# Eight experts' second product as three fp32r terms, with both operands split into a high and a low part

## The reference

```python
topw, topi = jax.lax.top_k(router_weights, K)          # K = 2 of E = 8 experts per token
h = jax.nn.gelu(jnp.einsum('td,edf->etf', xf, w1) + b1[:, None, :], approximate=False)
eo = jnp.einsum('etf,efd->etd', h, w2) + b2[:, None, :]  # the experts' second product
out = jnp.einsum('etd,te->td', eo, combine)
```

## Time and profile before

| | |
|---|---|
| median of 3 runs | 2344.29 us (2343.64 to 2345.33) |
| the profiled execution | 2352.8 us |
| its span, first to last instruction | 2351.0 us |
| stage B within the span | about 1401 to 1922 us |
| TensorE, VectorE, ScalarE, GpSimd busy | 91%, 64%, 46%, 41% of the span |
| mean granted TensorE clock | 0.98 |

### The profile page before, as it was taken

The page is one execution under the profiler, slowest core; times in us unless marked ns, Lnnn a source line. Parts: engine busy times, 40 slices in busy tenths (PEclk is TensorE's granted clock), DMA queues, the critical chain, the costliest instruction groups (busy, mean ns, idle before and its releaser), DMA issues.

```text
span 2351.0 us, 81509 instructions
## 1 busy us (share of the span) xinstructions
PE 2131.1 (91%) x31188; PEld 1835.3 (78%) x31189; DVE 1514.2 (64%) x3179; ACT 1086.2 (46%) x2772; POOL 961.8 (41%) x1190
## 2 busy tenths in 40 slices
PE   5999999999999999999999939999999977888887
PEld 4878877878878778778778739999999965666665
DVE  4687787787787886887877851111111127999997
ACT  2354354454454453543543525555555534444444
POOL 3445455454554553654654531000000015656663
PEclk9999999999999999999999969999999999999999
DMA  8401001001001010010000044111111121111110
GB/s 201 152 3 39 10 18 41 11 19 35 16 19 31 20 32 13 20 37 8 21 21 6 19 143 142 36 36 36 38 36 36 36 61 47 57 47 54 56 52 18
DMA packets 93810, 101.00 MB, mean 43 GB/s; under 512 B 24304, under 2 KB 84720, under 8 KB 93424
## 3 DMA queue, kind: packets, MB, share of 16 engines
q1 hardware_dynamic: 83728, 69.93, 9.9%
q0 software_dynamic: 9440, 27.29, 3.6%
q10 hardware_dynamic: 384, 0.01, 0.0%
HBM read 64.95 MB, written 32.24 MB: 41 GB/s over the span
## 4 chain that ended last, share of the span: by engine, by line
PE 54%; issue 17%; DVE 14%; POOL 6%; ACT 5%; SPq 1%; DMA 1%; DVEq 1%; POOLq 0%; ACTq 0%
PE ps_scores L1049 11%; PE ps_w L1059 10%; PE ps_o L875 7%; PE ps_scores L836 4%; ACT pt_all L1202 4%; PE ps_qk L723 4%; PE ps_qk L757 3%; PE ps_xv L663 2%; DVE rs L1448 2%; PE ps_xv L741 2%; DVE lower L1429 2%; POOL lower L1857 2%; POOL rstd L1873 1%; PE ps_scores L783 1%; PE ps_scores L843 1%
## 5 line engine op out<-in xcount | busy, mean ns | idle before, releaser
L1441 DVE TENSOR_REDUCE mb<-ps_scores 128x16 bf16<-128x2048 f32 x160 | 365.8, 2286 | 43.8 <-PE ps_scores L816 39.8
L1956 POOL DMA_INDIRECT arena<-sorted_y,pidx x64 | 63.9, 998 | 609.1 <-ACT pidx L1313 584.4
L1448 DVE RECIPROCAL rs<-ps_o 128x256 f32<-128x256 f32 x160 | 280.4, 1753 | 31.3 <-PE ps_o L875 27.2
L1202 ACT ACTIVATE pt_all<-ps_scores 128x512 f32<-128x512 f32 x512 | 264.2, 603 | 65.2 <-PE ps_scores L843 63.4
L1049 PEld LDWEIGHTS ps_scores<-tiles,w_now 128*128 128x128 f32 x2272 | 266.1, 193 | 5.4 <-issue 1.8
L1049 PE MATMUL ps_scores<-tiles,w_now 128*128 128x128 f32 x2272 | 266.6, 276 | 1.2 <-DVE tiles L1717 1.2
L1287 ACT ACTIVATE tiles<-ps_scores,b1s 128x128 f32<-128x128 f32 x568 | 154.5, 383 | 238.4 <-PE ps_w L1059 230.9
L1059 PE MATMUL ps_w<-arena,tiles 128*128 x1136 | 257.0, 379 | 2.5 <-ACT tiles L1287 2.5
L1059 PEld LDWEIGHTS ps_w<-arena,tiles 128*128 128x128 f32 x1136 | 210.3, 190 | 28.6 <-issue 2.9
L1873 POOL TENSOR_TENSOR rstd<-ve,neghalf 128x1 f32<-128x1 f32 x192 | 109.9, 572 | 274.1 <-DVE ve L1459 266.3
L1857 POOL TENSOR_TENSOR lower<-lower,consts 128x512 fp32r<-128x512 f32 x160 | 171.3, 1070 | 117.9 <-DVE lower L1429 77.6
(11 more groups left out here) (233 smaller groups left out, 4531.5 us busy)
## 6 DMA issues: line engine op xcount, KB each, us to landing
tiles<-sorted_x SPq DMA_DIRECT2D x72, 128.0 KB, 2.0
sorted_y<-tiles SPq DMA_DIRECT2D x71, 128.0 KB, 1.7
w_experts<-in_L_xattn_e_w SPq DMA_DIRECT2D x6, 1024.0 KB, 11.7
arena<-in_L_xattn_e_w POOLq DMA_DIRECT2D x12, 384.0 KB, 4.1
ct_scratch<-cT SPq DMA_DIRECT2D x32, 128.0 KB, 1.7
x_scratch<-x2b_all SPq DMA_DIRECT2D x32, 128.0 KB, 1.8
arena<-x_scratch SPq DMA_DIRECT2D x32, 128.0 KB
cT<-ct_scratch SPq DMA_DIRECT2D x32, 128.0 KB, 2.1
```

Source lines behind the costliest of these rows:

```text
L1202: nc.scalar.activation(pt[:, 4 * g:4 * g + 4, :].rearrange("p h q -> p (h q)"), ps_s[:, g, :], ACT.Exp, bias=bias, scale=LAYER[l]["scale"] ...
L1441: V.tensor_reduce(mb[:].rearrange("p (g r) -> p g r", g=BANKS)[:, :, 0:SLOTS], ps_s[:].rearrange("p g (h k) -> p g h k", h=SLOTS), AX_X, A ...
L1448: V.reciprocal(rs[:], ps_o[:, 2:4, :]).then_inc(recip_ready, 1)
```

## The change

Each operand of the second product becomes a sum of two fp32r numbers, high and low. A product is then high times high, plus high times low of the weights, plus low times high of the weights; low times low is left out. `down` has 24 fp32r matmuls for the 8 fp32 ones.

- Inner values: per tile, `tile_split` on VectorE makes `g_split` with two copies (the high halves) and two subtractions (the low halves), each of 128x512 elements.
- Second weights: per expert, `split_w2` on GpSimd makes the two parts with 4 copies of 128x512 and 8 subtractions of 128x256. The source is one raw buffer, the target a ring of two experts. From expert 2 on, GpSimd waits until the last tile that used this half of the ring is behind (`upto`).
- `hidden` waits for the split of the tile before, where it waited for its `down`.
- The raw weights of expert 0 are loaded inside stage A's last iteration. Those of expert e+1 are loaded when expert e is split.
- The first weights of experts 6 and 7 are loaded from SyncE's queue, between the first tile loads.
- The table has three more instructions (which half of the ring, which first weights to wait for, how many tiles up to each expert).

```diff
         def down(k):
             e = pe.value_load(tbi[0:1, 1, bass.ds(k, 1)], min_val=0, max_val=E - 1)
-            wait(pe, ld_experts, e * 48 + 16)
-            wait(pe, b_gelu, k + 1)
+            odd = pe.value_load(tbi[0:1, 3, bass.ds(k, 1)], min_val=0, max_val=1)
+            wait(pe, w2_ready, e + 1)
+            wait(pe, b_split, k + 1)
             wait(pe, b_y, k)
             for j in range(FC):
-                last = mm(ps_w[:, 0:D], gT[:, j, :], w2f[:, bass.ds(e * (FC * D) + j * D, D)], start=j == 0, stop=j == FC - 1)
+                for g_, w_ in ((0, 0), (0, 1), (1, 0)):
+                    last = mm(ps_w[:, 0:D], g_split[:, g_, j, :].bitcast(F32R),
+                              w2_split[:, bass.ds(odd * (2 * FC * D) + (w_ * FC + j) * D, D)].bitcast(F32R),
+                              start=j == 0 and g_ + w_ == 0, stop=j == FC - 1 and g_ == 1)
             last.then_inc(b_down, 1)
...
+        pe.wait_ge(table_step, TABLE_PAR)
...
         def hidden(k, par):
             wait(act, b_up, k + 1)
             wait(act, b_b1, k + 1)
-            wait(act, b_down, k)
+            wait(act, b_split, k)
...
+        def tile_split(k):
+            wait(dve, b_gelu, k + 1)
+            wait(dve, b_down, k)
+            half = FC // 2
+            for h in range(2):
+                V.tensor_copy(g_split[:, 0, half * h:half * (h + 1), :].bitcast(F32R), gT[:, half * h:half * (h + 1), :]).then_inc(b_high, 1)
+            for h in range(2):
+                wait_apart(dve, b_high, 2 * k + h + 1)
+                last = V.tensor_tensor(g_split[:, 1, half * h:half * (h + 1), :].bitcast(F32R), gT[:, half * h:half * (h + 1), :],
+                                       g_split[:, 0, half * h:half * (h + 1), :], ALU.subtract)
+            last.then_inc(b_split, 1)
...
                 tile_y(k - 1, (d - 1) % 2, j)
+                tile_split(k)
...
+        def split_w2(e):
+
+            pool.wait_ge(ld_w2, 16 * (e + 1))
+            if e >= 2:
+                tiles_ = pool.value_load(upto[0:1, e - 2:e - 1], min_val=1, max_val=TILES + 1)
+                wait_apart(pool, b_split, tiles_)
+            at_ = (e % 2) * 2 * FC * D
+            for j in range(0, FC, 2):
+                G.tensor_copy(w2_split[:, at_ + j * D:at_ + (j + 2) * D].bitcast(F32R), w2_raw[:, j * D:(j + 2) * D]).then_inc(w2_high, 1)
+            for j in range(FC):
+                if j % 2 == 0:
+                    pool.wait_ge(w2_high, FC // 2 * e + j // 2 + 1)
+                last = G.tensor_tensor(w2_split[:, at_ + (FC + j) * D:at_ + (FC + j + 1) * D].bitcast(F32R), w2_raw[:, j * D:(j + 1) * D],
+                                       w2_split[:, at_ + j * D:at_ + (j + 1) * D], ALU.subtract)
+            last.then_inc(w2_ready, 1)
+            pool.wait_ge(w2_ready, e + 1)
+
+        split_w2(0)
+        load_w2(1)
+        split_w2(1)
+        pool.wait_ge(table_step, TABLE_PAR)
         for e in range(2, E):
-            for j0, j1 in ((0, 3), (3, 6), (6, FC)):
-                load_w2(e, j0, j1)
-            pool.wait_ge(ld_experts, 16 + 48 * e)
+            load_w2(e)
+            split_w2(e)
```

SyncE's queue (the first weights of experts 6 and 7), and GpSimd's early load:

```diff
         load_tile(0, 0)
         load_tile(1, 1)
+        for s in range(NS):
+            sp.wait_ge(x2_stored[s], 16 * ITERS)
+        load_w1(W1_EARLY)
...
         tile_pair(0, True)
+        for e in range(W1_EARLY + 1, E):
+            sp.wait_ge(ld_w1, 16 * e)
+            load_w1(e)
...
+            if last and tau == TPI - 7:
+
+                pool.wait_ge(wo_ready, NT - 2 * NS)
+                pool.dma_start(w2_raw[:].rearrange("p (j n) -> p j n", j=FC),
+                               a["L2_xattn_e_w2"][0].rearrange("(j p) n -> p j n", p=P)).then_inc(ld_w2, 16)
```

More of the change, by code:

```diff
@@ L127, in program @@
     x2b_all = sb("x2b_all", [2816])
+    with nc.sbuf_tensor("w2_raw", [P, FC * D], F32) as w2_raw, nc.sbuf_tensor("w2_split", [P, 2 * 2 * FC * D], F32) as w2_split, \
+            nc.sbuf_tensor("g_split", [P, 2, FC, P], F32) as g_split:
+        pass
     arena = sb("arena", [16384])
@@ L198, in program @@
     w1f = w1[:].rearrange("p e c n -> p (e c n)")
-    w2f = arena[:, :]
     cv = Carver(arena)
@@ L288, in program @@
     tb = xT_all[:].rearrange("p a b c -> p (a b c)")[:, 0:5 * TILES].rearrange("p (a b) -> p a b", a=5)
-    tbi = sb("tbi", [3, TILES + 1], I32)
+    tbi = sb("tbi", [5, TILES + 1], I32)
+    upto = sb("upto", [E], I32)
     tails = sb("tails", [E], I32)
@@ L309, in program @@
     ld_w1 = sem("ld_w1")
-    ld_experts = sem("ld_experts")
+    ld_w2 = sem("ld_w2")
+    w2_ready = sem("w2_ready")
+    w2_high = sem("w2_high")
+    b_high = sem("b_high")
+    b_split = sem("b_split")
     ld_b2 = sem("ld_b2")
@@ L597, in _, with load_w1 @@
         load_tile(1, 1)
+        def load_w1(e):
+            sp.dma_start(w1[:, e], a["L2_xattn_e_w1"][e].rearrange("(c p) n -> p c n", p=P)).then_inc(ld_w1, 16)
+        for s in range(NS):
+            sp.wait_ge(x2_stored[s], 16 * ITERS)
+        load_w1(W1_EARLY)
         def tile_pair(j, first):
@@ L620, in _ @@
         sp.wait_ge(b_down, TILES)
+        sp.wait_ge(w2_ready, E)
         sp.dma_start(win_f, a["consts"][:, C_WIN:C_ALL]).then_inc(ld_window, 16)
@@ L1276, in copy_weights @@
             e = act.value_load(tbi[0:1, 1, bass.ds(k, 1)], min_val=0, max_val=E - 1)
-            wait(act, ld_experts, e * 48 + 16)
+            late = act.value_load(tbi[0:1, 4, bass.ds(k, 1)], min_val=W1_EARLY - 1, max_val=E - 1)
+            wait(act, ld_w1, late * 16 + 16)
             wait(act, b_up, k - 1)
@@ L1698, in _ @@
         tlink(V.tensor_copy(tbi[:, 1, TILES:TILES + 1], tbi[:, 1, TILES - 1:TILES]))
+        tlink(V.tensor_scalar_max(tbi[:, 4, 0:TILES + 1], tbi[:, 1, 0:TILES + 1], float(W1_EARLY - 1)))
         tlink(V.tensor_copy(tbi[:, 2, TILES - 3:TILES], tbi[:, 0, TILES - 1:TILES].to_broadcast([P, 3])))
@@ L1702, in _ @@
         assert step[0] == TABLE_ALL
+        tlink(V.tensor_scalar(tbi[:, 3, 0:TILES + 1], tbi[:, 1, 0:TILES + 1], 1, None, ALU.bitwise_and))
+        tlink(V.tensor_scalar_add(upto[:], incl, 1.0))
+        assert step[0] == TABLE_PAR
         tlink(V.tensor_scalar(shift[:], n_t, float(P), -float(SPAN), ALU.mult, ALU.add))
@@ L1731, in _ @@
         tile_evac(1, 1)
+        tile_split(0)
         def tile_pair(j):
@@ L1738, in tile_pair @@
                 tile_y(k - 1, (d - 1) % 2, j)
+                tile_split(k)
         pairs(tile_pair, dve)
         tile_y(TILES - 1, 0, (TILES - 1) // 2)
+        V.memset(ssq[:], 0.0).then_inc(b_split, 1)
+        dve.wait_ge(w2_ready, E)
         dve.wait_ge(ld_l3, 16 * 11)
@@ L1931, in _, with load_w2 @@
         pool.wait_ge(xr_ready, NT)
[L1933 to L1944, removed]
+        def load_w2(e):
+            pool.dma_start(w2_raw[:].rearrange("p (j n) -> p j n", j=FC),
+                           a["L2_xattn_e_w2"][e].rearrange("(j p) n -> p j n", p=P)).then_inc(ld_w2, 16)
+        def split_w2(e):
[17 more added lines that the diff above has]
+        pool.wait_ge(table_step, TABLE_PAR)
         for e in range(2, E):
-            for j0, j1 in ((0, 3), (3, 6), (6, FC)):
-                load_w2(e, j0, j1)
-            pool.wait_ge(ld_experts, 16 + 48 * e)
+            load_w2(e)
+            split_w2(e)
         def gather(n):
@@ L2003 @@
 TABLE_TAILS = 1
-TABLE_ALL = TABLE_TAILS + 6 + 1 + 3 * E + 8
-TABLE_POS = TABLE_ALL + 2 + 2 * (E - 1)
+TABLE_ALL = TABLE_TAILS + 6 + 1 + 3 * E + 9
+TABLE_PAR = TABLE_ALL + 2
+TABLE_POS = TABLE_PAR + 2 + 2 * (E - 1)
 _NAMES = ["L0_xattn_wv", "L0_xattn_wk", "L0_xattn_wq", "L0_xattn_w_out", "L0_xattn_b_out", "L0_xattn_g1",
```

## The result

Before and after ran side by side on one chip, four times each: 2344.81 us (2343.64 to 2349.14) before, 2327.73 us (2327.20 to 2331.94) after. The ratio is 0.9919 with a 95% interval of 0.9905 to 0.9933: a gain of 17 us, clear of the noise but small, 0.8%. The forecast was 2304, so less than half of its 40 us arrived. The profiled execution took 2331.94 us, its span is 2330.0, where the span before was 2351.0: 21 us.

What follows compares the result with a forecast made beforehand. TensorE was taken to bound the kernel in stage B; matmuls -52, meeting with GpSimd +13, start -2 and ends +1 gave -40 us, from the median 2304 us, own range 2290 to 2318, wide range 2280 to 2334.

Steps and rivals of the forecast that it cites:

- What bounds the kernel: Stage B: TensorE has no idle time, so a microsecond less of its time a tile shortens the stage equally.
- the matmul term: Stage B's `down`: 3.45 to 2.71 us a tile, 52 us less over 70 steady tiles (40 to 57).
- The pace by issue: Rival, chance 0.25: register addresses or table reads slow `down` to 2.98 us or start it 0.3 late; 2330 us.
- the meeting with GpSimd: Stage B: GpSimd's weight split delays VectorE's split, costing TensorE 1.3 us in each of 10 tiles, +13 us.
- Load not hidden: Rival, chance 0.09: fp32r matmuls in `down` do not hide their weight load or stream twice; 5.2 us, 2466 us.
- VectorE's split: Per tile in stage B: 2.35 us (2.2 to 2.8), hidden by `up` with 0.6 us to spare.
- GpSimd's split: Per expert in stage B: splitting the second weights takes about 9.4 us and holds VectorE up.
- The start: Start of stage B: earlier loads bring the first tile sooner, partly held back by GpSimd's first split; -2 us.
- a full start: Start of stage B: tile 0 could be in by 1396, for -5 us.
- The ends: First and last tiles of stage B: uncovered splits and table links, less a shorter last `down`; +1 us.

Runs made afterwards that it cites:

- Table first: Against the changed kernel, GpSimd starts expert 0's split only when VectorE's table is complete; 2328.97 us, ratio 0.9879 to the kernel before.

## Why the prediction was right or wrong

**What bounds the kernel: right.** TensorE stays busy through stage B, and a shorter `down` shortens the tile one for one.

**The failed step is the matmul term, by its size.** It put a full fp32r matmul at "the larger of 0.107 and 0.110" and `down` at 2.71 us. Measured are 0.120 and 2.97, just above 24 x 0.120 = 2.88, the upper bound that the L836 rows had given and that was set aside as "nearer to the load". The difference of 0.26 us over 70 tiles is 18 us, the largest miss: 24 x (0.120 - 0.113) = 0.17 is the pace, and 0.10 the first gap of 0.22. The steady gain is 34 us for 70 tiles and not 52. The measured 2327.7 us lies above the forecast's own range (2290 to 2318) for this reason above all, and inside the wide one (2280 to 2334), which holds most of the next rival. The reasoning failed at one point: that an fp32r column streams at the clock as an fp32 one does. fp32 columns take 0.216 / 512 = 0.42 ns. fp32r columns take 0.120 / 256 = 0.47 and 0.233 / 512 = 0.46 ns. Why they are a tenth slower no run tells.

**The pace by issue: nearly its time, another cause.** The rival gave 2330 and a `down` of 2.98, and both came out. But its cause, the register for each matmul, holds for 0.1 us of the tile only; the rest is the pace of the columns. That its time came out is luck: it had 18 us for the meeting with GpSimd, which cost 6, and nothing for stages A and C.

**Load not hidden: wrong, as forecast.** 24 matmuls of 128 columns at 0.112 us, of 256 at 0.120, and 16 loads for 24 changing `down` by 0.07 us show loads under matmuls on the same rows; as a sum of load and stream, 128, 256 and 512 columns could not give 0.112, 0.120 and 0.233. The rule of the Trainium skill, "TensorE: Matmul & The Clock Gate", Part 3, that a load overlaps only another row group, is contradicted by these three runs.

**VectorE's split: right.** 0.75 + 1.29 = 2.04 us for two copies and two subtractions, for 2.35 forecast. It ends 2.7 us after `up` began, for 3.2, with 1.1 us of slack for 0.6.

**GpSimd's split: right in length, the meeting too large.** 2.28 us for the 4 copies and 6.82 for the 8 subtractions are 9.1 us for 9.4. The prediction let it meet ten tiles at 1.3 us. It meets six at 0.97, and a seventh a little, 6.1 us for 13: GpSimd is released by VectorE's `g_split` [the page after], so it begins right behind a split of VectorE, and 9.1 us from there reach only one next split. The slack was 0.5 larger too. The Trainium skill, "SBUF — State Buffer", section "SBUF: two separate sides", says that the port pair is locked for one whole instruction. The tiles agree in kind (3.85 us for 2.04). A wait for one of GpSimd's subtractions (about 0.7 us) would not explain the 5.98 us of one instruction of VectorE's: there the wait spanned all eight.

**The start: wrong sign.** -2 forecast, +1.9 measured. The load was judged rightly: the first transposes come 3.8 us earlier in three profiles of four. The meeting was not. VectorE's small instructions beside GpSimd's first split lost 5.6 us over eleven of them in one profile and 5.8 in a single one in another, so evac and the first `up` came no earlier than before (23.5 us after `tails` in three profiles, for 23.5 to 23.8), and 2.3 later in the fourth. Behind that, the first split of VectorE met GpSimd's split of expert 1, and TensorE waited 1.4 to 1.8 us ahead of the first `down` in those three profiles. The tile of the first `up` also ran at a lower granted clock (0.59 to 0.70, for 0.63 to 0.76 before). The prediction had 0.8 for this split, under the ends, and no meeting there. Table first puts the start at -5 (32.2 for 37.4), which is the value given for a full start.

**The ends: near.** +1 forecast, -0.3 measured from the 71st `up` to the last y; the uncovered split(0) lies inside the start's +1.9. In the profile shown the last `down` took 4.64 us at a granted clock of 0.64, in another 3.14 at 1.00; the prediction had nothing for this.

**Sum.** Forecast -52 + 13 - 2 + 1 = -40. Measured, by the same terms: -34 + 6 + 2 + 0 = -26 (up to the last y), and +1.4 and +2.2 in stages A and C, where nothing was forecast. The matmuls missed by 18 and the start by 4; the meeting, 7 better by luck of where GpSimd's split begins, and the ends, 1 better, hid a part of that. Stages A and C add 3.6.

## What to carry to other kernels

Where two bounds of a price come from rows of another shape, take the one whose data type is the same, not the one whose mechanism is tidier: here it was 18 us. Before an engine is given work beside VectorE, look at what small, serial chain runs there; moving GpSimd's first split behind the table gave the start 7 us, of which 2 showed in the launch. And a split that must be finished under another engine's matmuls wants a second buffer, so that it begins when its input is there and not when the reader is through: with the table first it took 9 us off the change.

## What the runs showed of the hardware

A full fp32r matmul with its own weight load takes 0.112 us with 128 moving columns, 0.120 with 256 and 0.233 with 512, at a granted clock of 1.00. Fixed addresses in place of a register for 24 matmuls save 0.1 us a tile. GpSimd's fp32r copy of 128x512 takes 0.57 us by itself; VectorE's takes 0.38 and its subtraction 0.64, and 0.75 to 0.9 and 1.2 beside GpSimd. One VectorE instruction of 0.2 us stood for 5.98 us beside a run of eight of GpSimd's.
